# Relational graph layer on one core: epilogue chunks laid out so that a partition of the output holds 8 nodes in a row, and two more chunks done ahead of the last tiles

## The reference, cut to what matters

```
h   = relu(layernorm(x))
W   = einsum('rb,bio->rio', comp, basis)
s   = segment_sum(h[src] * weight, etype * N + dst)      # per relation and node
agg = relu(einsum('rni,rio->no', s, W) + bias)
res = relu(h @ res_w.T + res_b)
y   = agg + res
out = x + (y - mean(y)) * rsqrt(var(y) + 1e-5) * gamma + beta     # mean, var over nodes
```

## Time and profile before

| | us |
|---|---|
| median of 3 runs | 1998.72 (1998.26 to 1999.53) |
| the profiled execution, own time | 1997.0 |
| its span in the trace | 1994.9 |
| POOL busy | 1476.3 (74%) |
| PE busy | 1618.3 (81%) |
| DVE busy | 928.8 (47%) |
| ACT busy | 920.2 (46%) |

### The profile page before, as it was taken

One profiled execution on the slowest core, in us unless ns is written; L12 is line 12 of the kernel. 1 busy time (PEld: TensorE's weight loads), 2 busy tenths in 40 slices (PEclk: granted clock), 3 DMA queues, 4 the chain that ended last, 5 costly groups with the idle time before them and its releaser, 6 DMA issues. The chain is left out here.

```text
span 1994.9 us, 36295 instructions
## 1 busy us (share of the span) xinstructions
PE 1618.3 (81%) x6553; PEld 827.2 (41%) x6553; DVE 928.8 (47%) x3199; ACT 920.2 (46%) x2171; POOL 1476.3 (74%) x1548
## 2 busy tenths in 40 slices
PE   4599999999999488888888888988998999745434
PEld 4243444443333255555544553543443434322222
DVE  6631111311110177777746773873856747324223
ACT  4587777777776755444424441542424333000002
POOL 6777777777777677777777777777777777777772
PEclk9999999999999755555575558558676575855556
DMA  9599999999999522222211221221212211111125
GB/s 188 205 400 404 407 405 400 405 406 406 405 401 406 172 54 49 49 49 50 49 39 38 54 44 33 49 49 29 53 38 43 45 34 38 29 28 28 28 51 114
DMA packets 134350, 308.05 MB, mean 154 GB/s; under 512 B 63725, under 2 KB 66836, under 8 KB 108803
## 3 DMA queue, kind: packets, MB, share of 16 engines
q1 hardware_dynamic: 72266, 236.64, 31.0%
q0 software_dynamic: 49088, 50.36, 12.4%
q10 hardware_dynamic: 12768, 18.71, 3.4%
HBM read 79.75 MB, written 225.83 MB: 153 GB/s over the span
## 5 line engine op out<-in xcount | busy, mean ns | idle before, releaser
L530 POOL DMA_INDIRECT shared<-z_table,idx_all x1022 | 979.3, 958 | 320.5 <-issue 251.3
L503 POOL DMA_INDIRECT acc<-in_x,idx_all x512 | 494.9, 967 | 162.7 <-issue 155.8
L1105 PE MATMUL zps<-wp,res 128*128 128x512 bf16 x2352 | 531.6, 381 | 37.2 <-ACT zst L553 27.4
L553 ACT ACTIVATE zst<-zps 128x512 f32<-128x512 f32 (+1 forms) x784 | 411.6, 601 | 149.1 <-DMA z_table<-zst 126.5
L1105 PEld LDWEIGHTS zps<-wp,res 128*128 128x128 bf16 x2352 | 219.1, 98 | 340.4 <-ACT zst L553 99.2
L1232 PE MATMUL mps<-res 128*128 128x160 f32 (+4 forms) x684 | 350.4, 616 | 4.2 <-issue 2.5
L1219 PE MATMUL aps<-shared 128*64 128x36 f32 (+10 forms) x1032 | 206.3, 317 | 147.2 <-DMA shared<-z_table,idx_all 84.5
L977 DVE TENSOR_SCALAR shared<-iota,rel_all,wgt_all 128x36 f32<-128x36 f32 (+10 forms) x1051 | 316.1, 328 | 2.1 <-issue 1.8
L675 ACT ACTIVATE res<-res,hw 128x64 f32<-128x64 f32 x512 | 175.4, 343 | 275.6 <-DVE hw L1003 121.8
L1219 PE MATMUL zps<-shared 128*64 128x36 f32 (+10 forms) x1012 | 200.3, 317 | 120.5 <-DMA shared<-z_table,idx_all 61.7
L1219 PEld LDWEIGHTS aps<-shared 128*64 128x64 f32 x1032 | 133.3, 192 | 336.8 <-issue 168.0
(11 more groups left out here) (154 smaller groups left out, 888.4 us busy)
## 6 DMA issues: line engine op xcount, KB each, us to landing
z_table<-zst SPq DMA_DIRECT2D x194, 1024.0 KB
wp<-z_table SPq DMA_DIRECT2D x2560, 0.2 KB
wp<-z_table ACTq DMA_DIRECT2D x1152, 0.2 KB
head_rows<-acc SPq DMA_DIRECT2D x64, 256.0 KB, 9.9
shared<-z_table,idx_all POOLq DMA_INDIRECT x1022, 2.5
res<-head_rows ACTq DMA_DIRECT2D x62, 256.0 KB
acc<-in_x,idx_all POOLq DMA_INDIRECT x512, 6.4
out_x<-zst SPq DMA_DIRECT2D x12, 256.0 KB
```

The lines of the kernel that those rows point to most:

```text
L503: e.indirect_dma_start(out=ring[:, b % NRING, i, :], out_offset=None, in_=x, in_offset=bass.IndirectOffsetOnAxis(ap=idx_all[:, t:t + 1], a ...
L530: e.indirect_dma_start(out=ys[:, q % NY, :], out_offset=None, in_=table[:, :], in_offset=bass.IndirectOffsetOnAxis(ap=idx_all[:, col:col + ...
L553: e.activation(to, frm, ACT.Copy).then_inc(s_ez, 1)
L1105: last = e.matmul(to, lhsT=stationary(px, pw), rhs=moving(px, pw), start=(a == 0), stop=(a == 2))
```

## The change

1. **Layout.** In chunk n, partition i of `xo` now holds 8 nodes in a row, from n*1024 + 8*i on (in the last chunk 2 nodes in a row, on 106 partitions). x is reloaded and the output written in pieces of 2 KB (512 bytes in the last chunk), one DMA for each of 13 chunks. To get there, `sum_halves` and `residual` read their moving operand with a step of 8 elements in `acc` (4-byte floats) and `xp` (bf16); before, they read blocks of 128 columns in a row. The transposes read `acc` as before. Both halves now hold the same number of nodes, so `moments` of the last chunk has one bn_stats in place of two.
2. **Two more early chunks.** Chunks 9 and 10 are done after the tiles 988 and 993, when the first 11264 nodes are complete (group 187); 2 chunks stay for the end. The flag has a second condition for it.
3. **The 8 instructions** that fill `wmean` and `wdiff` move from the end to before the flag's wait on DVE.
4. **Fetched rows.** ACT_BATCH is 14, ACT has 3 buffers, and ACT's tiles are placed 30 tiles after the place in `sums` where their last row is issued: 135, 223, 351, 439, 567, 719, 847, 935, 983 (before: 199, 327, 463, 591, 727, 855, 935, 975, 1023). SP's are 20 as before, some of them 8 tiles on or back; POOL's remain 1022. ACT issues all rows that are left ahead of `shifted(9)`.

```
-DONE_GROUP, DONE_NODES, DONE_STEP = 176, 9216, 5
+DONE, DONE_STEP = ((176, 9), (187, 11)), 5
-ACT_BATCH, ACT_REST, ACT_EPI, ACT_TILES, NACT = 13, 64, 10, 9, 2
+ACT_BATCH, ACT_REST, ACT_EPI, ACT_TILES, NACT = 14, 64, 10, 9, 3
+ACT_LATE = 30
...
+    epi_run = [2 * w // P for w in epi_width]
...
+            def in_runs(rows, n):
+                n0, n1, run = n * EPI, min((n + 1) * EPI, N), epi_run[n]
+                return rows[n0:n1, :].rearrange("(i j) f -> i (j f)", j=run), xoflat[0:(n1 - n0) // run, n0 // P * F:(n0 // P + run) * F]
...
+            for n in range(NEPI):
+                rows, frm = in_runs(out, n)
                 e.wait_ge(s_oc, n + 1)
-                e.dma_start(ov[:, t0:t1, :], xo[:, t0:t1, :]).then_inc(s_out, 16)
-            e.dma_start(out[(NT - 1) * P:N, :], xo[0:LAST, NT - 1, :]).then_inc(s_out, 16)
+                e.dma_start(rows, frm).then_inc(s_out, 16)
...
                 for n in range(EPI_EARLY):
+                    if n == done_from[1]:
+                        fetch_rows(ACT_TILES * P)
                     shifted(n)
                     fetch_rows(ACT_EPI)
-                fetch_rows(ACT_TILES * P)
...
# residual
-                            lambda px, pw: xp[:, ch, px, 0:tiles * P].rearrange("p (t a n) -> p t a n", a=2, n=P)[:, :, h, :])
+                            lambda px, pw: xp[:, ch, px, 0:nodes].rearrange("p (i q a) -> p a q i", a=2, q=run // 2)[:, h])
# sum_halves
-                both = acc[:, n * EPI:n * EPI + 2 * w].rearrange("p (t a n) -> p t a n", a=2, n=P)
+                both = acc[:, n * EPI:n * EPI + 2 * w].rearrange("p (i q a) -> p a q i", a=2, q=epi_run[n] // 2)
```

More of the change, by code:

```diff
@@ L88, in rgcn_kernel @@
     unit_end = [n for n, (_, _, k, size) in enumerate(seq) if k == size - 1]
[L91 to L112, removed]
     def window(u):
@@ L125, in rgcn_kernel @@
     NEPI = math.ceil(NT * P / EPI)
-    EPI_EARLY = DONE_NODES // EPI
     epi_width = [min(BANK, NT * P // 2 - n * BANK) for n in range(NEPI)]
-    done_unit = (DONE_GROUP - HG) * NU - 1
-    epi_after = [unit_end[done_unit] + (n + 1) * DONE_STEP for n in range(EPI_EARLY)]
-    assert DONE_NODES % EPI == 0 and epi_after[-1] + NOH + 1 < NZT
+    done_from = [0] + [chunks for _, chunks in DONE]
+    done_unit = [(group - HG) * NU - 1 for group, _ in DONE]
+    EPI_EARLY = done_from[-1]
+    epi_after = [unit_end[done_unit[k]] + (n + 1) * DONE_STEP
+                 for k in range(len(DONE)) for n in range(done_from[k + 1] - done_from[k])]
+    assert epi_after == sorted(epi_after) and epi_after[-1] + NOH + 1 < NZT
+    epi_run = [2 * w // P for w in epi_width]
+    TAIL_ROWS = (N - (NEPI - 1) * EPI) // epi_run[-1]
+    assert N % 2 == 0 and (N - (NEPI - 1) * EPI) % epi_run[-1] == 0 and epi_run[-1] == 2 and BANK % epi_run[0] == 0
     DUMP = NT * P
@@ L152, in rgcn_kernel, with tile_of_row @@
     assert done == len(head_items)
+    tile_at_factor, tile_now = [], 0
+    for kind, t, *_ in sums:
+        if kind == "tile":
+            tile_now = t
+        elif kind == "factor":
+            tile_at_factor.append(tile_now)
+    def tile_of_row(n):
+        if n < ACT_BATCH * NHB:
+            return tile_at_factor[n // ACT_BATCH]
+        return HEAD_UNTIL + (n - ACT_BATCH * NHB) * 0.36
+    owner, pooled, nsp, nact = {}, 0, 0, 0
+    for u, tiles in enumerate(units[:-NU]):
+        pooled += len(tiles)
+        if u % NU < NU - 1:
+            continue
+        if nact < ACT_TILES and unit_end[u] >= tile_of_row((nact + 1) * P - 1) + ACT_LATE:
+            owner[unit_end[u]] = ("act", nact)
+            nact += 1
+            pooled -= 1
+        elif pooled >= SP_FIRST + SP_EVERY * nsp:
+            owner[unit_end[u]] = ("sp", nsp)
+            nsp += 1
+            pooled -= 1
+    assert nact == ACT_TILES
+    tiles_of_queue = {q: [t for t in sorted(owner) if owner[t][0] == q] for q in ("sp", "act")}
+    pool_tiles = [t for t in range(NZT) if t not in owner]
+    pool_nth = {t: q for q, t in enumerate(pool_tiles)}
+    for a in range(NACT, ACT_TILES):
+        assert tiles_of_queue["act"][a - NACT] < tile_of_row(a * P)
     table = nc.dram_tensor("z_table", [NCLS * N * CLS, F], F32)
@@ L212, in rgcn_kernel @@
         wcopy = zst[:, NZS - 1, :, :].rearrange("p t n -> p (t n)").rearrange("p (r f) -> p r f", f=F)
[L213 removed]
+        xoflat = zflat[:, 0:NT * F]
+        xo = xoflat.rearrange("p (t f) -> p t f", f=F)
         sacc = zflat[:, 0:SUM_NODES * HALF]
@@ L232, in rgcn_kernel @@
         chunk_f = sb("chunk_f", [1, NHK])
-        over = sb("over", [1, 2 * NHK + NU * len(WINS)])
+        over = sb("over", [1, 2 * NHK + NU * len(WINS) + len(DONE)])
         hm = sb("hm", [P, 2, 3, HB])
@@ L464, in _ @@
             table_landed(e)
[L465 to L470, removed]
+            def in_runs(rows, n):
+                n0, n1, run = n * EPI, min((n + 1) * EPI, N), epi_run[n]
+                return rows[n0:n1, :].rearrange("(i j) f -> i (j f)", j=run), xoflat[0:(n1 - n0) // run, n0 // P * F:(n0 // P + run) * F]
+            whole, run = (NEPI - 1) * EPI, epi_run[0]
+            e.dma_start(xoflat[:, 0:whole // P * F].rearrange("p (c r) -> p c r", c=NEPI - 1),
+                        x[0:whole, :].rearrange("(c i j) f -> i c (j f)", c=NEPI - 1, j=run)).then_inc(s_xre, 16)
+            rows, to = in_runs(x, NEPI - 1)
+            e.dma_start(to, rows).then_inc(s_xre, 16)
+            for n in range(NEPI):
+                rows, frm = in_runs(out, n)
                 e.wait_ge(s_oc, n + 1)
-                e.dma_start(ov[:, t0:t1, :], xo[:, t0:t1, :]).then_inc(s_out, 16)
-            e.dma_start(out[(NT - 1) * P:N, :], xo[0:LAST, NT - 1, :]).then_inc(s_out, 16)
-            e.wait_ge(s_out, 16 * (math.ceil(NT / 8) + 1))
+                e.dma_start(rows, frm).then_inc(s_out, 16)
+            e.wait_ge(s_out, 16 * NEPI)
         @block.gpsimd
@@ L801, in stats_of_groups @@
             def stats_of_groups():
-                spans = over[:, 2 * NHK:].rearrange("p (h k) -> p h k", h=NU)
+                spans = over[:, 2 * NHK:2 * NHK + NU * len(WINS)].rearrange("p (h k) -> p h k", h=NU)
+                undone = over[:, 2 * NHK + NU * len(WINS):]
                 e.tensor_copy(base_i[:, :].rearrange("p (g h) -> p h g", h=NU),
@@ L807, in stats_of_groups @@
                 e.wait_ge(s_me, len(METAS))
-                e.tensor_reduce(flag_f[:, 0:1], base_i[:, done_unit + 1:NGZ * NU], AX, ALU.min)
+                for k, u in enumerate(done_unit):
+                    last = e.tensor_reduce(undone[:, k:k + 1], base_i[:, u + 1:NGZ * NU], AX, ALU.min)
+                link(last)
+                for k, (_, chunks) in enumerate(DONE):
+                    e.tensor_scalar(undone[:, k:k + 1], undone[:, k:k + 1], -1.0, float(chunks * EPI), ALU.mult, ALU.add)
                 for k, w in enumerate(WINS):
@@ L811, in stats_of_groups @@
                 link(last)
[L812 to L815, removed]
+                link(e.tensor_reduce(flag_f[:, :], over[:, :], AX, ALU.max))
+                e.tensor_scalar(flag_i[:, :], flag_f[:, :], 0.0, None, ALU.is_le).then_inc(s_flag, 1)
             def tiles_of(a):
@@ L899, in moments @@
                 e.wait_ge(s_ey, n + 1)
[L900 to L904, removed]
+                e.bn_stats(bst[:, n, :], y if n < NEPI - 1 else y[:, 0:TAIL_ROWS]).then_inc(s_bst, 1)
+            e.wait_ge(s_cst, 5)
+            for h, sign in ((0, 1.0), (1, -1.0)):
+                for to, factor in ((wmean, 0.5), (wdiff, sign)):
+                    for k in range(2):
+                        e.tensor_scalar(to[h * F:(h + 1) * F, k * F:(k + 1) * F], stack2[h * F:(h + 1) * F, :], factor, None, ALU.mult)
             flag = fast_path_flag(e)
@@ L1026, in _ @@
                 moments(n)
[L1028 to L1032, removed]
             e.wait_ge(s_bst, NEPI)
@@ L1037, in _ @@
             link(e.tensor_tensor(bmv[:, 9:10], bmv[:, 2:3], bmv[:, 2:3], ALU.mult))
-            e.scalar_tensor_tensor(out=bmv[:, 3:4], in0=bmv[:, 9:10], scalar=(N - upper) * upper / N / N,
+            e.scalar_tensor_tensor(out=bmv[:, 3:4], in0=bmv[:, 9:10], scalar=0.25,
                                    in1=bmv[:, 1:2], op0=ALU.mult, op1=ALU.add).then_inc(s_st, 1)
@@ L1174, in sum_halves @@
                 w = epi_width[n]
-                both = acc[:, n * EPI:n * EPI + 2 * w].rearrange("p (t a n) -> p t a n", a=2, n=P)
+                both = acc[:, n * EPI:n * EPI + 2 * w].rearrange("p (i q a) -> p a q i", a=2, q=epi_run[n] // 2)
                 for h in range(2):
-                    last = e.matmul(halves_psum(n)[h * F:(h + 1) * F, 0:w], lhsT=stack2[:, :], rhs=both[:, :, h, :],
+                    last = e.matmul(halves_psum(n)[h * F:(h + 1) * F, 0:w], lhsT=stack2[:, :], rhs=both[:, h],
                                     start=True, stop=True)
```

17 lines of the change are left out of this document (10 added, 7 removed).

## The result

| | before | changed |
|---|---|---|
| median of 19 runs, us | 1996.96 | 1994.12 |
| lowest and highest | 1995.36 to 1999.53 | 1989.66 to 1996.85 |
| the profiled execution: own time, span | 1997.0, 1994.9 | 1994.12, 1992.1 |

The ratio is 0.9983 (95% interval 0.9976 to 0.999): 3.4 us faster, by 2.0 to 4.8; the two medians differ by 2.8. I had forecast 7.5 us. By the line of 0.2% that the prediction drew, 3.4 us is still "the same", to which it had given 0.11, though the interval leaves no doubt of the sign. In a later job beside other kernels the ratio was 0.9978 (0.9969 to 0.9987). Differences in us between kernels are worked out from such ratios, or from single traces where the text says so.

What follows compares the result with a forecast made beforehand. POOL's gathers bound the stage, then a tail with output in 256-byte pieces. DVE's last addition, 1985.53 - 2.48 + 1.0 = 1984.05, plus 2.8 and 0.5 gave span 1987.4, 7.5 us less; median 1991.2, range 1987.5 to 1995.5.

Steps and rivals of the forecast that it cites:

- POOL ends where it did: Gather stage: POOL never waits for a buffer, and its last gather still starts at 1959.5.
- Output: Kernel end: with 2 KB pieces the span ends 3.3 us after DVE's last addition, not 9.4; gain 6.1 us.
- rival C: Output no faster, still about 216 GB/s: gain 2.4 us, median 1996.3; chance 0.17 including DMA rates in between.
- rival B: Last chunk's 106-partition DMA runs on few engines: end 1.8 us later, median 1993.0; even odds within main forecast or shared-limit alternative.
- 8 small instructions and two chunks: Tail: moved instructions and two fewer late chunks bring bn_aggr 4.19 us sooner, if PE's part costs the same.
- Step of 8 in `sum_halves`: Tail on PE: both halves share one read limit, 3.41 us in place of 1.71 for the first late chunk.
- rival A: Column halves share no limit, or bf16 is untouched: gain 10.3 us, median 1988.4; chance 0.33.
- Residual: Start of stage on PE: 150 matmuls take 31.4 us, not 8.22, so SP goes on 17.6 us later.
- Reload over the last gathers: Stage end: delayed reload of x runs from 1954.6 to 1962.6, over the last gathers; costs 1.0 us (0 to 3).
- PE's lag, ring and tile 983: Gather stage: PE's lag reaches about 25 tiles, under 36; its 6 us wait for ACT's tile 983 is covered.
- Clock: Tail on PE: the clock may stay at the lower level, costing up to 2.6 us over 13 chunks.

Runs made afterwards that it cites:

- the probe: Changed kernel with 20 groups of matmuls at various operand steps added behind PE's last transposes, on a slow chip; no time or ratio of its own given.
- reload early: Changed kernel with the reload of x moved between SP's 17th and 18th tile, residual still at step 8; ratio to before 0.9961.
- last DMA split: Changed kernel with the last chunk's output in two DMAs, of 96 and 10 partitions; ratio to before 0.9971.
- three mends: Changed kernel with residual at step 2 and ACT reordering, reload after SP's 17th tile, last output DMA as 96 and 10 partitions; ratios to before 0.9956 and 0.9959.
- the run with 9 early chunks: Changed kernel with 9 early chunks in place of 11, so 4 late chunks; ratio to before 0.9987.

## Why the prediction was right in sign and range, and its gain twice too large

The span is 4.7 us above the forecast (1992.1, not 1987.4): 2.8 from POOL's later end, 2.5 from the reload over the gathers and 1.1 from the last DMA, less 1.6 for the step in `sum_halves`, which cost less than I took. So an error in my favour hid part of those against me. By its own steps:

- *POOL ends where it did* (0). It ended 2.8 us later in this execution. By the ten traces that is mostly the luck of an execution; whether the changed kernel's stage is a little longer on average stays open. The traces less POOL show 5.6 us, the ratios 3.4 and 4.4.
- *Output* (a gain of 6.1 of 9.4). e is 4.35, not 3.3. The pieces are as fast as I took them to be: 385 GB/s where the earlier trace rows had 216, so rival C is out. What is missing is the last DMA, 1.1 us, which I had kept as rival B and not in the sum.
- *8 small instructions and two chunks* (4.19 with PE at no extra cost). c fell from 8.88 to 4.80, by 4.08: right.
- *Step of 8 in `sum_halves`* (1.71 dearer): this step failed, and rival A was right here. 2.08 us, not 3.4. The limit is 1.7 to 1.8 ns for a column and half. At the clock of 0.50 a float instruction takes 0.85 us for 512 columns anyway, 1.67 ns each, so the step is almost hidden. I had read the same 1.7 ns as 0.83 for each of four reads, and doubled it for two halves; the first is a wrong count of reads, the second a guess.
- *Residual* (31.4 us): 33.05 measured. That was luck: the two errors cancel where the operand is bf16, for each column is paid once there (150 matmuls of mostly 256 columns in pairs: 0.44 us a pair, the 0.45 of the probe). SP's start at 688 (690.2) and the reload near 1954.6 (1956.8) came out right with it. The granted clock fell from 1.00 to 0.50 at about 662 us and the pace stayed (32 matmuls in the 7 us below, 0.44 us a pair, as in the probe at 1.00), so the clock isn't the cause:
```profile
663.00:670.00 7.00, 7.00 (x32) 2.37 (x30) 0.00 (x0) 1.37 (x2) 0.94 (x1) 0.50 0.57 201
```
- *Reload over the last gathers* (1.0 us, bounds 0 to 3): this is the term that was mis-sized most. b grew by 3.53. I let the reload end at 1962.6 and the last gather land just before. But it went at 345 GB/s, started at 1956.8, and was through only at about 1968; gathers landed up to 6.0 us after their issue, and PE got the last five between 1965.06 and 1968.33. The share of that row (0.99) says that the DMA engines were full. The step that failed is the overlap: beside the reload a gather didn't land in the 2.5 us that it takes alone, so the last one, issued at 1962.27, landed at 1968.3 and not near 1965.
- *PE's lag, ring and tile 983*: POOL stood never more than 0.32 us between two gathers, as worked out, though ACT's clearing and SP's rows began 20 us late. PE waited 4.0 us for tile 983, not 6.
- *Clock* (up to 2.6 us dearer): it cost next to nothing, since two parts cancel. From the scaling to DVE's last addition the changed kernel took 10.61 us at a granted clock of 0.73, the kernel before 10.25 at 0.77. From bn_aggr to the scaling it took 2.99 us at 0.83, the kernel before 3.40 at 0.50. Over the ten traces this stretch is 2.99 us in the four in which the clock had risen to 0.74 or more (the changed kernel twice, reload early, last DMA split) and 3.40 in the six at 0.50. The three mends are among the six, so they lost 0.6 to 0.7 us in d. PE was busy with late tiles just before in the four, but also in the run with 9 early chunks, which is at 0.50; so what raises the clock there stays open.

The Trainium skill's rule on the number of DMA engines ("DMA: Bandwidth & Descriptors", under why a DMA increments its semaphore by 16) agrees with the rows: with 106 partitions the last two microseconds ran at 38 and 13 GB/s, the first of them with a share of 0.14, 2.2 engines of 16, and with 96 and 10 they are gone.

The Trainium skill's rule on SBUF's 16-byte lines ("SBUF — State Buffer", under Door 1) is that each access to a new line pays, and that two accesses to a line are enough for full speed. In floats the probe agrees: 256 columns cost 0.226 us at a step of 2 (two columns in 16 bytes), about what they cost without a step at full clock (0.43 us for 512, from 1966.37 to 1966.80 in the kernel before's last full late chunk), and 0.453 at a step of 4. In bf16 it doesn't: a step of 4 also puts two columns in 16 bytes and costs 0.22 us against 0.11. The same section lets four floats and eight bf16 be stepped for free; in both the probe has a cost, and the measurement decides. One price fits all groups: 1.7 to 1.8 ns for each 16 bytes that a matmul instruction touches (256 columns at a step of 4 bf16 or 2 floats touch 128 of them, 0.22 us; at 8 bf16 or 4 floats and more 256 of them, 0.43 to 0.46 us).

## What to carry to other kernels

A layout moved from a DMA to a matmul's operand was paid where the operand was bf16 (33 us for 8), and hardly where it was float at the low clock (2.08 us for 1.98); look for an engine that reads PSUM, which did the same reordering for nothing. When a stage starts late under a queue that has no slack (SP here), follow that queue to its last item: its lateness came out 1270 us on, as a 3 MB reload over the last gathers. And give a bulk transfer a place where the ring covers it, not the end of the list.

## What the runs showed of the hardware that I had not expected

- A stepped moving operand costs 1.7 to 1.8 ns a column for each column half by itself, two halves side by side at no more (0.444 us for one bf16 matmul, 0.45 for a pair), at a granted clock of 1.00 as at 0.50. ACT's read of PSUM with a step of 4 floats costs 0.06 us in 7.9.
- The length of 1022 equal gathers, never waiting, varied between 1286.7 and 1295.1 us, and the median gather was 944 ns in some executions and 947 in others, of one kernel too.
- A DMA of 106 partitions at the end of the output ran at a share of 0.14, 2.2 of 16 engines, and cost 1.1 us against the same bytes as 96 and 10 partitions.
- In one job a chip ran the kernel before at 3146.8 us, and in a later job the same chip ran it at 2000.27. In the first, SP's row fetches took 0.83 us each in place of 0.49. The cause stays open.
